# Routed experts of a decoder layer: gate and up weights copied to a ring and held stationary, one transpose per tile fewer

## The reference

```python
def _L0_ffn_ref(x, Wr, Wg, Wu, Wd, Sg, Su, Sd):
    E, K, F = (16, 2, 128)
    FS = 256
    ...
    shared = jax.nn.silu(xf @ Sg) * (xf @ Su) @ Sd
    probs = jax.nn.softmax(xf @ Wr, axis=-1)
    topk_p, topk_i = jax.lax.top_k(probs, K)
    cw = jnp.zeros((T, n_exp), x.dtype).at[jnp.arange(T)[:, None], topk_i].add(topk_p)

    def step(acc, ew):
        wg, wu, wd, c = ew
        y = jax.nn.silu(xf @ wg) * (xf @ wu) @ wd
        return (acc + y * c[:, None], None)
    routed, _ = jax.lax.scan(step, jnp.zeros_like(xf), (Wg, Wu, Wd, cw.T))
    return (routed + shared).reshape(b, s, d)
```

## Time and profile before

| | us |
|---|---|
| median of 3 runs | 637.95 |
| lowest and highest | 637.26, 642.2 |
| the profiled execution, device time | 638.39 |
| its span in the profile | 636.6 |
| mean granted clock of TensorE in it | 0.953 |

### The profile page before, as it was taken

How to read it: one execution, slowest core, us unless ns; L and a number is a source line. 1 busy time by engine, 2 the same in 40 slices (tenths; PEclk the granted TensorE clock), 3 DMA queues, 4 the chain that set the end, 5 groups by cost and what they waited for, 6 DMA issues and landing times.

```text
span 636.6 us, 14211 instructions
## 1 busy us (share of the span) xinstructions
PE 560.8 (88%) x4551; PEld 304.6 (48%) x4552; DVE 381.2 (60%) x1031; ACT 384.7 (60%) x530; POOL 212.9 (33%) x238
## 2 busy tenths in 40 slices
PE   3996999999999999999998999999789589999920
PEld 2442333333333333333366777676355366666610
DVE  5787555655555555555553788878466634444436
ACT  3587899999999999999954556453200023333311
POOL 4000791692079100000013422803737024444420
PEclk9998999999999999999999999999789789999965
DMA  9923333444444433433226400000212134444358
GB/s 255 353 78 69 72 73 73 75 79 77 77 76 76 76 74 73 73 73 72 58 81 194 125 3 2 1 2 2 102 52 102 41 92 129 127 126 132 100 165 272
DMA packets 53547, 60.20 MB, mean 95 GB/s; under 512 B 10721, under 2 KB 44642, under 8 KB 53506
## 3 DMA queue, kind: packets, MB, share of 16 engines
q1 hardware_dynamic: 47570, 47.24, 31.1%
q0 software_dynamic: 3792, 10.36, 4.5%
q10 hardware_dynamic: 2144, 2.10, 1.0%
HBM read 22.17 MB, written 18.61 MB: 64 GB/s over the span
## 4 chain that ended last, share of the span: by engine, by line
PE 74%; DVE 11%; issue 5%; ACT 4%; DMA 3%; another core or an unknown queue 1%; DVEq 1%; SPq 0%; POOL 0%; ACTq 0%; POOLq 0%
PE ps L711 20%; PE ps L701 19%; PE ps L1098 8%; PE ps L1113 3%; PE ps L753 2%; PE ps L854 2%; PE ps L922 2%; PE ps L720 2%; PE ps L1090 2%; DVE ftmp L1742 2%; DMA val<-y_tok 2%; PE ps L1002 1%; PE ps L989 1%; PE ps L629 1%
## 5 line engine op out<-in xcount | busy, mean ns | idle before, releaser
L1598 DVE TENSOR_TENSOR ps<-ps,kstack 128x128 f32<-128x128 f32 (+3 forms) x256 | 123.6, 495 | 103.3 <-PE ps L701 103.2
L1244 ACT ACTIVATE pT<-ps 128x1024 f32<-128x1024 f32 x128 | 124.9, 1023 | 7.3 <-PE ps L701 2.7
L701 PE MATMUL ps<-qstack,kstack 96*128 96x512 bf16 x352 | 93.0, 387 | 4.5 <-issue 4.5
L711 PE MATMUL ps<-pT,vcur 128*32 128x256 f32 x1024 | 80.5, 387 | 0.0
L1244 ACT ACTIVATE xn<-ps 128x1024 f32<-128x1024 f32 x64 | 65.5, 1024 | 9.0 <-PE ps L701 8.1
L582 POOL DMA_INDIRECT y_tok<-ftmp,dest_i x47 | 45.2, 961 | 73.1 <-DVE ftmp L2015 72.5
L1244 ACT ACTIVATE xnT<-ps 128x1024 f32<-128x1024 f32 x64 | 65.2, 1019 | 0.2
L1098 PE MATMUL ps<-parts,xnT 128*128 x188 | 54.1, 413 | 6.0 <-issue 5.9
L701 PEld LDWEIGHTS ps<-qstack,kstack 96*128 96x128 bf16 x352 | 29.1, 98 | 54.7 <-issue 15.5
L1403 ACT ACTIVATE oT<-ps 128x128 f32<-128x128 f32 x47 | 13.0, 278 | 63.1 <-PE ps L1098 58.1
L556 POOL TENSOR_TENSOR resid<-resid,projb 128x512 f32<-128x512 f32 x8 | 10.1, 1267 | 121.6 <-DVE xn L1937 121.0
(11 more groups left out here) (300 smaller groups left out, 973.1 us busy)
## 6 DMA issues: line engine op xcount, KB each, us to landing
qstack<-parts SPq DMA_DIRECT2D x132, 64.0 KB, 2.3
x_slots<-wcur SPq DMA_DIRECT2D x1, 6016.0 KB, 20.2
kT<-x_slots SPq DMA_DIRECT2D x47, 128.0 KB
kstack<-parts SPq DMA_DIRECT2D x132, 32.0 KB, 2.0
early<-parts SPq DMA_DIRECT2D x60, 64.0 KB, 2.3
resid<-in_x_dram SPq DMA_DIRECT2D x4, 512.0 KB, 7.8
parts<-in_L_ffn_Wg_dram SPq DMA_DIRECT2D x16, 128.0 KB, 2.3
parts<-in_L_ffn_Wu_dram SPq DMA_DIRECT2D x16, 128.0 KB, 2.3
```

Of the source, the lines that this page charges most:

```text
L701: nc.tensor.matmul(ps[:, score_bank(g3, kt) + g, :], kstack[g3][:, kt * P:(kt + 1) * P], qstack[g3][:, 1 - first, 512 * g:512 * (g + 1)], ...
L711: mm = nc.tensor.matmul(ps[2 * HD * g:2 * HD * (g + 1), 6 + r, 0:256], vcur[:, r, kt, :], pT_ring[kt % 4][:, 256 * g:256 * (g + 1)], start ...
L1244: nc.scalar.activation(pT_ring[kt % 4], two_banks(score_bank(g3, kt)).rearrange("p a n -> p (a n)"), ACT.Exp, bias=-SHIFT).then_inc(s_exp, 1)
L1598: nc.vector.tensor_tensor(blk, blk, within[:, side, 4 * P - n:] if side == 0 else within[:, side, 0:n], ALU.mult)\
```

## The change

The orientation of the gate and up product is turned round: the weights are the stationary operand and the 128 columns of the transposed tile move, so the product comes out with the hidden index on the partitions, as the down product needs it. `tile_hidden_transpose` (PE) and `tile_hidden_in` (DVE) go. A tile's gate and up are now four matmuls of 128 columns instead of two of 256.

The stationary operand is not read from a register's address: for each tile SP reads the offset from `owner_i` and copies the expert's 4 x 128 columns from `wflat` to one of four buffers `wring` (in the memory `val`, free once the scatter has landed), 256 KB from SBUF to SBUF. `tile_down` still reads its weights at a register's address. The loads of tiles 4 to 46 move from SP's queue to ACT's.

The owners are formed after `accumulate(1)` rather than after the last hot; `ended_by(0)` goes ahead of `choices(1)`. PE does 26 of the 32 destination products before the first transposes and 6 after the first gate and up, and waits for `s_acc` and `s_dest` later. The semaphores `s_x` are used again for the weight copies under the name `s_in`, `s_hT` and `s_hT_ps` go.

```diff
+        wring = [val[:].rearrange("p t d -> p (t d)")[:, r * 4 * F:(r + 1) * 4 * F] for r in range(4)]
...
             def load_tile(j):
-                after(sp, s_tT_ps, j - 3)
                 sp.dma_start(xt[j % 4], x_slots[j * P:(j + 1) * P, :]).then_inc(s_xt[j % 4], 16)
 
+            def load_weights(j):
+
+                w = sp.value_load(owner_i[0:1, j:j + 1], min_val=0, max_val=(E_ROUTED - 1) * WCOLS)
+                after(sp, s_tgu, j - 3)
+                sp.dma_start(wring[j % 4], wflat[:, ds(w, 4 * F)]).then_inc(s_in[j % 4], 16)
+
+            sp.wait_ge(s_wres, 48 * E_ROUTED)
+            sp.wait_ge(s_owner, 1)
             for r in range(4):
                 sp.wait_ge(s_scatter[r], 16 * PAIRS // 4)
             for j in range(SLOT_TILES):
-                load_tile(j)
+                if j < 4:
+                    load_tile(j)
+                load_weights(j)
...
-            destinations()
+            destinations(0, PAIRS - 6)
...
-            def tile_gate_up(j, r, w):
+            def tile_gate_up(j, r):
 
                 pe.wait_ge(s_tT, j + 1)
+                pe.wait_ge(s_in[r], 16 * (j // 4 + 2))
                 after(pe, s_thid, j - 1)
-                for k in range(KD):
-                    mm = nc.tensor.matmul(ps[:, 2 + r % 2, 0:2 * F], xtT[r][:, k, :],
-                                          wflat[:, ds(w + k * 2 * F, 2 * F)],
-                                          start=(k == 0), stop=(k == KD - 1))
+                for m in range(2):
+                    for k in range(KD):
+                        mm = nc.tensor.matmul(ps[:, 2 + r % 2, m * F:(m + 1) * F], wring[r][:, (2 * k + m) * F:(2 * k + m + 1) * F],
+                                              xtT[r][:, k, :], start=(k == 0), stop=(k == KD - 1))
                 mm.then_inc(s_tgu, 1)
 
-            def tile_hidden_transpose(j, r):
+            def tile_down(j, r, w):
 
                 pe.wait_ge(s_thid, j + 1)
-                after(pe, s_hT, j - 1)
-                nc.tensor.transpose(ps[:, 4 + r % 2, 0:F], hid_s[r % 2], ident[:]).then_inc(s_hT_ps, 1)
...
             pe.wait_ge(s_wres, 48 * E_ROUTED)
-            pe.wait_ge(s_acc, NCHUNK)
-            pe.wait_ge(s_dest, 1)
             for j in range(3):
                 tile_transposes(j, j)
-            tile_gate_up(0, 0, tile_weights(0))
+            pe.wait_ge(s_owner, 1)
+            tile_gate_up(0, 0)
+            destinations(PAIRS - 6, PAIRS)
+            pe.wait_ge(s_acc, NCHUNK)
             tile_steps(0, 4)
...
+            def load_tile(j):
+
+                if j < SLOT_TILES:
+                    nc.scalar.dma_start(xt[j % 4], x_slots[j * P:(j + 1) * P, :]).then_inc(s_xt[j % 4], 16)
...
                 if j + 3 < SLOT_TILES:
                     tile_in(j + 3)
+                    load_tile(j + 7)
...
             accumulate(1)
...
+            nc.vector.tensor_copy(owner_i[:], owner[:]).then_inc(s_owner, 1)
+            hots(8, 18)
+            hidden(3, 0)
+            hidden(3, 1)
+            accumulate(2)
+            hots(18, PAIRS)
+            accumulate(3)
```

More of the change, by code:

```diff
@@ L221, in decoder_layer @@
         xtT = [xnT[:].rearrange("p k q -> p (k q)")[:, r * D:(r + 1) * D].rearrange("p (k q) -> p k q", k=KD) for r in range(4)]
-        hT = [oT[:, 1, r * F:(r + 1) * F] for r in range(2)]
+        wring = [val[:].rearrange("p t d -> p (t d)")[:, r * 4 * F:(r + 1) * 4 * F] for r in range(4)]
         hid_s = [oT[:, 1, (2 + r) * F:(3 + r) * F] for r in range(2)]
@@ L275, in decoder_layer @@
         hid = [oT, att_c[:].rearrange("p t d -> p (t d)").rearrange("p (a n) -> p a n", a=KD)]
-        s_x = [sem(f"s_x{c}") for c in range(NCHUNK)]; s_out = sem("s_out")
+        s_in = [sem(f"s_in{c}") for c in range(NCHUNK)]; s_out = sem("s_out")
         s_wkv_in = sem("s_wkv_in"); s_wq_in = sem("s_wq_in")
@@ L311, in decoder_layer @@
         s_xt = [sem(f"s_xt{r}") for r in range(4)]; s_tT_ps = sem("s_tT_ps"); s_tT = sem("s_tT"); s_tgu = sem("s_tgu")
-        s_tsilu = sem("s_tsilu"); s_thid = sem("s_thid"); s_hT_ps = sem("s_hT_ps"); s_hT = sem("s_hT")
+        s_tsilu = sem("s_tsilu"); s_thid = sem("s_thid");
         s_ty_ps = sem("s_ty_ps"); s_yt = sem("s_yt"); s_yst = [sem(f"s_yst{r}") for r in range(4)]
@@ L364, in load_x @@
             def load_x(c):
-                sp.dma_start(resid[:, c * CT:(c + 1) * CT, :], x_d[:, c * CT:(c + 1) * CT, :]).then_inc(s_x[c], 16)
+                sp.dma_start(resid[:, c * CT:(c + 1) * CT, :], x_d[:, c * CT:(c + 1) * CT, :]).then_inc(s_in[c], 16)
             load_x(0)
@@ L1066, in _, with destinations @@
             down(3)
-            def destinations():
+            def destinations(first, last):
                 pe.wait_ge(s_place, 2 * TOPK)
-                for n in range(PAIRS):
+                for n in range(first, last):
                     i = pair_of(n)
@@ L1075, in destinations @@
                                           start=(n == 0), stop=(n == PAIRS - 1))
-                mm.then_inc(s_dest_ps, 1)
-            destinations()
+                if last == PAIRS:
+                    mm.then_inc(s_dest_ps, 1)
+            destinations(0, PAIRS - 6)
             def tile_weights(j):
@@ L1123, in tile_steps @@
                         w[i + 1] = tile_weights(j + 1)
-                        tile_gate_up(j + 1, (i + 1) % 4, w[i + 1])
-                    tile_hidden_transpose(j, i % 4)
+                        tile_gate_up(j + 1, (i + 1) % 4)
                     if not peeled or j + 3 < SLOT_TILES:
@@ L1453, in chunk_stats @@
                 tiles = slice(c * CT, (c + 1) * CT)
-                dve.wait_ge(s_x[c], 16)
+                dve.wait_ge(s_in[c], 16)
                 for t in range(tiles.start, tiles.stop):
@@ L1955, in _ @@
             place_parts(0)
-            hots(0, 4)
+            ended_by(0, early_owner[:])
             choices(1)
@@ L1962, in _ @@
             accumulate(0)
-            hots(4, 12)
+            hots(0, 8)
             hidden(2, 0)
@@ L1966, in _ @@
             accumulate(1)
-            ended_by(0, early_owner[:])
-            hots(12, 20)
-            hidden(3, 0)
-            hidden(3, 1)
-            accumulate(2)
-            hots(20, 28)
-            accumulate(3)
-            hots(28, PAIRS)
             ended_by(1, owner[:])
@@ L2003, in tile_hidden @@
                 dve.wait_ge(s_tsilu, j + 1)
-                after(dve, s_hT_ps, j - 1)
+                after(dve, s_ty_ps, j - 1)
                 nc.vector.tensor_tensor(hid_s[r % 2], silu_s[r % 2], ps[:, 2 + r % 2, F:2 * F], ALU.mult).then_inc(s_thid, 1)
-            def tile_hidden_in(j, r):
-                dve.wait_ge(s_hT_ps, j + 1)
-                after(dve, s_ty_ps, j - 1)
-                nc.vector.tensor_copy(hT[r % 2], ps[:, 4 + r % 2, 0:F]).then_inc(s_hT, 1)
             def tile_result(j, r):
@@ L2020, in _ @@
                     tile_hidden(j + 1, j + 1)
-                tile_hidden_in(j, j)
                 if j > 0:
```

14 lines of the change are left out of this document (6 added, 8 removed).

## The result

| | before | after |
|---|---|---|
| median, first chip (17 runs each) | 639.73 us | 634.86 us |
| ratio, 95% interval | | 0.9933 [0.9911, 0.9954] |
| span of the profiled execution | 636.6 us | 632.9 us |
| median on another chip (fifth experiment) | 621.98 us | 628.07 us |
| its ratio, 95% interval | | 1.0066 [1.0034, 1.0097] |

What follows compares the result with a forecast made beforehand. It took PE's sequencer and array, nearly even, to bound the tiles, with a separate approach before them. 638.39 less 5.5 (approach), 4.8 (loop) and 0.6 (end) gave 627.5 profiled, 627.3 as median; range 620.5 to 636 us.

Steps and rivals of the forecast that it cites:

- What bounds the kernel now: Whole kernel: DMA bandwidth not short; PE's sequencer sets the tiles' pace, nearly even with the array in a 1.75 us step.
- Both give 0.10 to 0.12: Tile loop: array and sequencer each save that many us a step; 0.11 over 44 steps makes 4.8 us.
- Rival 1: Tile loop: the sequencer keeps the pace and the loop gives nothing, 632.1 us; sign "issue" before gate passes; chance 0.17.
- Gate and up: Tile step on PE: eight passes of 128 columns with weight loads fetched ahead take 0.88 us.
- rival 5: Gate and up on PE: the weight loads lie open, 2.43 us a step, about 650 us; chance 0.03.
- Sequencer's part: PE's sequencer in a tile step: loses one register step and one wait, at least 0.10 us, keeping all 61 register loads.
- Copies hidden on SP and DMA: Tile loop: weight copies cost nothing, SP's 0.95 to 1.65 us fitting the step; DMA about 0.9 us a copy.
- rival 4: Tile loop: DMA engines become the bound at 2.27 us a step, PE waiting for copies, 640.7 us; chance 0.08.
- Approach: Ahead of the tiles' steady loop: earlier owners and transposes bring the third gate and up forward, 5.5 us, bounds 4.8 to 6.1.
- the hole: Before the tiles: a 6.06 us wait of every engine but GpSimd, taken to stay and cover 2.1 us of moved VectorE work.
- the 4 us named: Approach, sign in the profile after: VectorE waits on the silu ahead of `hidden(3, 1)` for 4 rather than 6 us.
- End: After the last gate pass: the last tile skips the removed transpose and copy, 0.6 us gained, bounds 0 and 1.

Runs made afterwards that it cites:

- fifth experiment: The changed kernel unedited, run again on another chip against the kernel before: 628.07 us, ratio 1.0066.
- e9: The kernel before with one edit, PE's register reads without the run-time bounds check: 609.96 us, ratio 0.9810 to the kernel before.
- e7: The changed kernel with PE's registers read four at a time, unchecked, and four tile loads ahead of the first weight copy: 599.95 us, ratio 0.9649 to the kernel before.
- e1: The changed kernel with SP copying 64 of a tile's 512 weight columns (timing only, results wrong): 611.49 us, ratio 0.9813 to the kernel before.
- e3: The kernel before with the change's weight copies on SP added, their result unused: 631.90 us, ratio 1.0131 to the kernel before.
- e12: The kernel before unedited, run again for its trace on another chip: 621.75 us, one run.
- e8: The changed kernel with the down weights also copied to a ring, so PE reads no register: 608.67 us, ratio 0.9814 to the kernel before.
- e13: The kernel before's orientation without weight copies, with early owners, split destinations and registers read in fours, unchecked: 605.02 us, ratio 0.9749 to the kernel before.

## Why the prediction was wrong, step by step

*What bounds the kernel now.* Half right. I named PE's sequencer as the pace and then called sequencer and array "nearly even", with an array of 1.63 to 1.75 us. The array's floors are 1.62 (e9) and 1.54 (e7); the kernel before stood 0.13 above its floor in the best steps and 0.42 in the mean.

*The step that failed* is "Both give 0.10 to 0.12": the gain of the loop, -4.8 us forecast, +3.8 measured. It took the register read at 0.31 us from the earlier trace rows into a kernel whose DMA traffic I had doubled myself. The read became 0.55 in the median and the reads of the 44 steps 15.2 us longer in all; e1 and e3 show the copies as the cause. Rival 1, that the sequencer keeps the pace, is the case that came true, for a reason it did not name, and it had the loop lose nothing where it lost 3.8. Its sign in the profile was the one given for it: "issue" ahead of PE's first gate pass.

*Luck in the number.* 634.6 us in the profiled execution, against 627.5, is 8.6 more in the loop, 1.6 more at the end and 3.1 less in the approach. That the time still lies within the range of 620.5 to 636 is owed to the first chip's approach. The idea for the loop was sound but for the copies' price: with narrow ones (e1) the 44 steps take 8.7 us less than in the kernel before (e12), where I had forecast 4.8.

*Gate and up* in eight passes: 0.89 us by their starts against 0.88. Right; rival 5 is out.

*Sequencer's part:* 0.25 shorter instead of 0.10. Mis-sized: all of it lies between the first weight load and the read (0.915 against 0.665), where two entries of the sequencer are gone. With the distances to the next one they took 0.27 us (545.54 to 545.81 in the kernel before), where I took 0.10 for all.

*Copies hidden on SP and DMA:* right as far as it goes. No wait of PE for `val`, share 0.77 within the 0.7 to 0.9 named. The copy's share is 0.77 x 2.19 - 0.85 = 0.84 us of the engines (0.90 by the time of its own packets), where I took 0.9; rival 4 is out, and e8 shows how near it was. The Trainium skill's page "SBUF — State Buffer", section "Door 1: The DMA port swizzle", gave 0.80 for 128 partitions, and by that the trace agrees. What I priced was the copy's time; what it cost was PE's register read, for which the sum had no term.

*Approach:* -8.6 against -5.5 (bounds 4.8 to 6.1). The mechanism held: the hole stayed (VectorE waits 491.1 to 494.9, the 4 us named), transposes start at 502.8, the granted clock between is 1.00 where it was 0.53. Three terms were too careful by 2.0 in all: `down(3)` began 1.0 earlier (496.3) and took 5.4 instead of 5.9, and the 26 products took 1.1 instead of 1.6; 1.1 more lie behind them. There my sum did not come out: its terms (0.9 to 1.8, 0.3 and 2) put the third gate and up at 509.2 to 510.1 and not at 509.7 to 511.0; measured are 3.5 us from the first gate and up to the third (503.81 to 507.28) where I had 4.3, with 1.8 for VectorE's address work. But most of this gain lives on the first chip's holes, which give VectorE free time to form the owners in.

*End:* +1.0 against -0.6. The last tile itself is shorter (the last down product 603.8 against 609.0, 2.9 us behind the last gate and up instead of 3.4); the rest is in reading back and adding, which spreads from 30.4 to 32.3 between the kernels here. It stays open.

## What to carry to other kernels

Where an engine's step ends in "issue", add up its sequencer's instructions before costing the array: here every register read cost 0.3 us at least, its bounds check 0.2 to 0.25, and dropping the check of an already clamped value gave more than the whole change of orientation. When an edit adds DMA traffic, list what else reads SBUF meanwhile, register reads of the sequencers included, and place them where the array has work queued. And a gain in an approach is to be checked on another chip: an order that fills a hole is worth little where the hole is missing.

## What the hardware showed that I had not expected

- A sequencer's register read of SBUF is slowed by copies in flight, on PE and on SP: on PE 0.30 us at least, up to 1.05 beside one 256 KB copy (1.1 us of packets), a median of 0.31 again with 32 KB; on SP 0.26 at least and 0.54 in the median of e3. Copies are not the only cause. In e9, which has none, nine reads took 0.53 to 0.72 beside tile loads and scatters, while others at a DMA share of 1.0 took 0.30; what tells these apart the runs don't show.

```profile
L1083 PEldq TENSOR_LOAD <-owner_i x61: 295/311/721, 495.6 to 579.7; - x61
```

- Four aligned neighbours come in one read of 0.33 us at best (e13, ten reads of 0.327 to 0.344), where one takes 0.30. The Trainium skill's page "Runtime: NRT & Kernel Launch", section "Instruction fetch mechanics", gives about 200 ns for each register even in bulk, and it speaks of registers loaded from HBM; by it four would be an estimated 0.8. For these reads from SBUF the trace is far below it, and the measurement decides.
- The kernel before is 15 to 19 us faster on four other chips than on the first. In the traces 16.4 of the 16.6 us between the spans are there by the last silu of the shared expert.
